# Batch 0's gate/up products switch to block products two units earlier, and a unit's five weight sums come from three VectorE operations

## The reference

```
base = x W^T                                   (1024 -> 1024)
y    = base + 2 * (x A_e^T * gates) B^T        (8 experts of rank 16, top 2 by biased logits)
gate = y Wg^T ; up = y Wu^T                    (1024 -> 3584)
h    = silu(gate) * up
out  = x + h Wd^T                              (3584 -> 1024)
```

## Time and profile before

| | |
|---|---|
| median of three runs | 1322.58 us (1322.0 to 1322.73) |
| span of the profiled execution, first to last instruction | 1320.3 us |
| median less that span | 2.3 us |
| PE busy | 1315.4 us, 8592 matmuls |
| DVE busy | 801.2 us (61%) |
| ACT, POOL busy | 405.1 us, 118.4 us |
| granted TensorE clock | 9 in all 40 slices of the page |
| moved by DMA | 287.58 MB |

### The profile page before, as it was taken

How to read it: one execution, slowest core, us unless ns; L and a number is a source line. 1 busy time by engine, 2 the same in 40 slices (tenths; PEclk the granted TensorE clock), 3 DMA queues, 4 the chain that set the end, 5 groups by cost and what they waited for, 6 DMA issues and landing times.

```text
span 1320.3 us, 22272 instructions
## 1 busy us (share of the span) xinstructions
PE 1315.4 (100%) x8592; PEld 863.2 (65%) x8592; DVE 801.2 (61%) x1581; ACT 405.1 (31%) x703; POOL 118.4 (9%) x156
## 2 busy tenths in 40 slices
PE   9999999999999999999999999999999999999999
PEld 7854566546666666676667666667666766666666
DVE  7889898788525587763733455555473254545613
ACT  4377755461102343421101233332110122222000
POOL 3200011150000011100000101100000011111000
PEclk9999999999999999999999999999999999999999
DMA  8479977216946788843884668553387355556564
GB/s 294 154 267 359 371 288 256 78 65 238 347 148 184 252 308 320 325 147 113 278 296 152 221 210 274 181 156 121 110 315 269 131 188 183 181 180 212 171 233 135
DMA packets 119609, 287.58 MB, mean 218 GB/s; under 512 B 15184, under 2 KB 18896, under 8 KB 118736
## 3 DMA queue, kind: packets, MB, share of 16 engines
q1 hardware_dynamic: 119216, 285.99, 62.7%
q10 hardware_dynamic: 288, 0.16, 0.0%
HBM read 241.80 MB, written 44.30 MB: 217 GB/s over the span
## 4 chain that ended last, share of the span: by engine, by line
PE 96%; DVE 2%; DMA 1%; issue 0%; SPq 0%; ACT 0%; DVEq 0%
PE banks L1072 26%; PE banks L1025 23%; PE banks L1095 14%; PE banks L1102 13%; PE banks L815 4%; PE banks L867 2%; PE banks L994 2%; PE banks L993 2%; PE banks L911 1%; PE banks L912 1%; PE banks L913 1%; PE banks L908 1%; PE banks L909 1%; PE banks L910 1%; PE banks L1131 1%; DMA mix_dram<-mixed 1%
## 5 line engine op out<-in xcount | busy, mean ns | idle before, releaser
L1072 PE MATMUL banks<-y_hi,gu_ring 128*128 128x512 f16 x1552 | 365.4, 379 | 0.0
L1072 PEld LDWEIGHTS banks<-y_hi,gu_ring 128*128 128x128 f16 x1552 | 151.8, 98 | 143.5
L1095 PE MATMUL banks<-h,piece 128*128 128x512 f16 x840 | 188.5, 379 | 0.0
L2031 ACT ACTIVATE sg<-banks,sc 128x512 f32<-128x512 f32 x112 | 76.8, 687 | 226.5 <-DVE banks L1757 165.4
L2272 POOL TENSOR_TENSOR m<-m,m 128x256 f32<-128x256 f32 x100 | 72.6, 726 | 821.2 <-DVE m L1738 815.1
L1095 PEld LDWEIGHTS banks<-h,piece 128*128 128x128 f16 x840 | 82.2, 98 | 89.8
L1760 DVE TENSOR_TENSOR banks<-banks,m 128x256 f32<-128x256 f32 x100 | 43.1, 431 | 133.5 <-PE banks L1072 133.3
L1102 PE MATMUL banks<-h,piece 128*128 128x256 f16 x896 | 106.2, 273 | 0.0
L1102 PEld LDWEIGHTS banks<-h,piece 128*128 128x128 f16 x896 | 87.7, 98 | 19.7
L1025 PE MATMUL banks<-y_lo,gu_ring 128*128 128x256 f16 x776 | 100.6, 273 | 0.0
L2159 ACT COPY m<-banks 128x256 f32<-128x256 f32 x100 | 36.8, 368 | 169.2 <-PE banks L1025 169.1
(11 more groups left out here) (258 smaller groups left out, 2006.8 us busy)
## 6 DMA issues: line engine op xcount, KB each, us to landing
piece<-down_dram SPq DMA_DIRECT2D x80, 448.0 KB, 5.8
mix_c<-mix_dram SPq DMA_DIRECT2D x84, 384.0 KB, 3.9
piece<-Wd SPq DMA_DIRECT2D x64, 448.0 KB, 5.5
gu_ring<-Wg SPq DMA_DIRECT2D x108, 256.0 KB, 3.2
gu_ring<-Wu SPq DMA_DIRECT2D x108, 256.0 KB, 3.0
mix_a<-mix_dram SPq DMA_DIRECT2D x84, 256.0 KB, 2.7
mix_dram<-mixed SPq DMA_DIRECT2D x28, 640.0 KB, 5.6
wb<-w_dram SPq DMA_DIRECT2D x64, 256.0 KB, 3.4
```

What stands on the lines that cost most here:

```text
L1072: mm = MM(bank, w[:, k, :], y_hi[:, k, :], start=False, stop=(k == KC - 1), skip_group_check=True)
L1095: mm = MM(bank, w[:, k, :], h[:, half * MH + k, 0, :], start=(start and k == 0), stop=False, skip_group_check=True)
L2031: S.activation(sg[:, n % SG, :], banks[:, chunk_bank(b, m, 0), :], ACT.Silu, scale=sc[:, b, 1:2]).then_inc(s_sg, 1)
```

## The change

- `PLAIN` becomes 10: units 10 and 11 of batch 0 go by block products too.
- `SUM_AT` is spread anew. Before, the sums of (units) were at s: 0:(0) 1:(1) 2:(2,3) 3:(4) 4:(5) 5:(6) 6:(7) 7:(8,9) 8:(10) 9:(11) 10:(12,13) and from 11 on s:(s+3). Now: 0:(0) 1:(1) 2:(2,3) 3:(4) 4:(5) 5:(6,7) 6:(8) 7:(9) 8:(10,11) and from 9 on s:(s+3).
- `weight_sums` has three additions or subtractions: one of 128x512 and two of 128x1024. For that the order of the last two sums is swapped and product 6's sum has the other sign (a1-b1), which `y_sum[:, 1]` takes up with a factor of -2. So the doubling of `y_sum` (one operation of 128x3072, in every batch) becomes two, of 128x2x1024 and 128x1024.

```
-    PLAIN = 12
-    SUM_AT = {0: (0,), 1: (1,), 2: (2, 3), 7: (8, 9), 10: (12, 13)}
-    SUM_AT.update({s: (s + 1,) for s in range(3, 7)})
-    SUM_AT.update({s: (s + 2,) for s in range(8, 10)})
-    SUM_AT.update({s: (s + 3,) for s in range(11, MC - 3)})
+    PLAIN = 10
+    SUM_AT = {0: (0,), 1: (1,), 2: (2, 3), 3: (4,), 4: (5,), 5: (6, 7), 6: (8,), 7: (9,), 8: (10, 11)}
+    SUM_AT.update({s: (s + 3,) for s in range(9, MC - 3)})
...
-                    fifth, seventh, sixth = (mix(n)[:, i] for i in range(2, 5))
+                    fifth, sixth, seventh = (mix(n)[:, i] for i in range(2, 5))
...
-                step(V.tensor_scalar(y_sum[:], y_sum[:], 2.0, None, ALU.mult))
+                step(V.tensor_scalar(y_sum[:, 0:3:2], y_sum[:, 0:3:2], 2.0, None, ALU.mult))
+                step(V.tensor_scalar(y_sum[:, 1], y_sum[:, 1], -2.0, None, ALU.mult))
...
                 even, odd = halved[:, 0], halved[:, 1]
-                a1, a2, b1, b2 = (w[:, i * KC // 2:(i + 1) * KC // 2] for w in (odd, even) for i in range(2))
+                left, right = (halved[:, :, i * KC // 2:(i + 1) * KC // 2] for i in range(2))
                 out = mix(s)
-                V.tensor_tensor(out[:, 0], a1, b2, ALU.add)
-                V.tensor_tensor(out[:, 1], b1, b2, ALU.add)
-                V.tensor_tensor(out[:, 2], a1, a2, ALU.add)
-                V.tensor_tensor(out[:, 3], a2, b2, ALU.subtract)
-                V.tensor_tensor(out[:, 4], b1, a1, ALU.subtract).then_inc(s_mix, 1)
+                V.tensor_tensor(out[:, 0], odd[:, 0:KC // 2], even[:, KC // 2:KC], ALU.add)
+
+                V.tensor_tensor(out[:, 1:3], left, right, ALU.add)
+
+                V.tensor_tensor(out[:, 3:5].rearrange("p c k j -> p (c k) j"), odd, even,
+                                ALU.subtract).then_inc(s_mix, 1)
```

More of the change, by code:

```diff
@@ L1057, in products_576 @@
                 if n < MC:
-                    fifth, seventh, sixth = (mix(n)[:, i] for i in range(2, 5))
+                    fifth, sixth, seventh = (mix(n)[:, i] for i in range(2, 5))
                 else:
                     pe.wait_ge(d_mix_c[n % 2], 16 * ((n - MC) // 2 + 1))
-                    fifth, seventh, sixth = (mix_c[:, n % 2, i] for i in range(3))
+                    fifth, sixth, seventh = (mix_c[:, n % 2, i] for i in range(3))
                 pe.wait_ge(s_34, nth(n))
```

## The result

The changed kernel takes 1324.47 us in the median of 18 runs (1323.09 to 1326.33), the kernel before 1321.97 us in 18 runs beside them (1321.55 to 1323.15). Forecast were 1325.2 us and a range from 1322.8 to 1327.0. The spans of the two profiled executions are 1322.4 and 1320.3 us. One thing in the times was not foreseen: those of before scatter over 1.6 us, those of after over 3.2 us.

A forecast was written before the change was run, and what follows sets the result against it. PE was taken as the bound, busy 1315.4 of 1320.3 us. Units -0.80, waits +3.29, +0.20, +0.27, old waits -0.21, -0.14 gave +2.6 us on 1322.6: 1325.2 us, range 1322.8 to 1327.0.

The forecast's parts named there:

- Part 1: Units 10 and 11 of batch 0 by block products: PE gains 0.80 us, 6.51 us a unit against 6.91.
- Parts 2 and 3: On DVE, a unit's sums get 0.14 us cheaper; the doubling of y_sum costs 0.19 us more once a batch.
- rival (b): DVE isn't late at the switch, as wide operations cost like narrow ones: -1.2 us, 1321.4 us; chance 6%.
- Part 4: At the new switch DVE starts y_blocks at 138.39, 2.6 us late, and PE stands 1.39 us.
- Part 5: At m45 of unit 10, unit 9's store, landing at 142.8, holds unit 12's sums: PE 3.29 us late with y_blocks' wait.
- part 7: Old waits for m45: the 0.21 us at 156.09 goes, the one at 195.53 shrinks by 0.14 us.
- Part 6: The next two units: PE waits 0.20 us for m45 of unit 11, then 0.27 us for ACT's copy.
- rival (a): Unit 9's store is in time, waits are 1.64 + 0.20 + 0.27: +0.96 us, 1323.5 us; chance 20%.
- rival (d): After PE's new waits the clock falls to 1.2 GHz for one unit: 6.5 us longer, 1331.7 us; chance 3%.
- (c): The DMA backlog doesn't drain, sums of units 13 and 14 wait too: +5.6 us, 1328.2 us; chance 11%.

The follow-up runs named there:

- e1: The kernel before with only the three-operation sums and the new doubling of y_sum, block products still from unit 12: 1321.68 us.
- e5: The changed kernel with unit 12's sums in a spare buffer and one down sum moved from step 8 to 9: 1323.20 us.
- e10: e9 with DVE making m45 of unit 10 ahead of unit 12's sums in step 9: 1323.22 us.
- e12: e9 with block products from unit 12 and the spread of the sums as in the kernel before: 1321.70 us.
- e6: The changed kernel with the last 1.75 MB of Wd issued two steps later, behind unit 9's store and unit 12's load: 1322.89 us.
- e2: The changed kernel, switch at unit 10, but with five operations of 128x512 for a unit's sums as before: 1325.51 us.
- e3: The changed kernel with unit 12's sums written to a spare buffer, so that they wait for no store: 1324.15 us.
- e4: The changed kernel with one down sum moved from step 8 to 9, and the next ones spread anew: 1324.23 us.
- e11: e6 with three operations into an unused buffer on DVE ahead of y_blocks of batch 0: 1325.83 us.
- e9: e8 with ACT taking its copies (copy_12) ahead of the silu in even steps of batch 0: 1321.48 us.
- e8: e6 with two down sums moved behind the switch to block products, and the later ones spread anew: 1321.79 us.

## Why the prediction was right

The time came out 0.7 us under the forecast, and the waits came where they were said to come. Of these 0.7 us, 0.6 lie in the starting point: the sum was put on 1322.6 us, from three runs of the kernel before, and the median of its 18 runs is 1321.97. As a difference, +2.5 us stand against +2.6. So good a match is partly luck, since one large term was off and two causes were not in the sum.

**Part 1, 0.80 us for two units.** It holds as far as it can be read: block units are 6.51 us apart in after, and the lost starts less the 0.74 us of before, and less 0.80 where the switch is at unit 10, meet the medians of e1, e5 to e10 and e12 within 0.4 us (e6: 2.60 - 0.74 - 0.80 = +1.06, measured +1.0). In e2, e3, e4, e11 and after the median lies 0.5 to 0.8 us off, to either side: these are the kernels whose landings or clock differ most between executions.

**Parts 2 and 3.** The value between the two bounds was right: 0.60 us for the 1024-wide sum, 2.27 us for a unit, 0.69 and 0.43 us for the doubling. That refutes rival (b), and the profile of e1 shows both parts at once.

**Part 4.** DVE was at the switch within 0.01 us of the forecast, and PE lost 1.40 us there, 1.39 predicted. This is the largest term of the result, and it came from adding up DVE's queue from a point that stays, where it waits for PE.

**Part 5** failed in size. The second wait was to be 1.9 us and PE lost 1.06. The forecast took the label of 0.21 us off to find when PE wants `m45`; the lost start there was 0.38, so the term should have been 2.07 us (the same 0.17 us is missing in part 7, and the sum is not changed by it). From 2.07 to 1.06 it is the store, which landed 1.0 us before the time taken. The idle stretch of the DMA engines that I counted on came (share 0.44 in the slice from 118 us, and 0.70 over 115.47 to 120.47, where the same 5 us of before have 0.85) and still this store was no later. The traces of after, e2, e3, e4 and e5 put this landing between 141.8 and 143.7 us, so 142.8 was a fair middle and a single number the wrong form: the profile of after shows one draw. What the term lacked was unit 12's load: in the profiles of e3 and e4 it held DVE for 1.5 and 1.6 us, in that of after it did not.

**Part 6** held: 0.19 us for `m45` of unit 11 (0.20), and 0.37 us for the copy (0.27 predicted; its label says 0.21).

**Part 7.** The wait that went was worth 0.38 us, not 0.21, because its label leaves out the overlap of matmuls. The other lost 0.14 us, as said (0.37 to 0.23).

**The sum** by lost starts is -0.80 + 1.40 + 1.06 + 0.19 + 0.37 - 0.38 - 0.14 = +1.70 us for the profiled execution, where +2.6 was forecast; that is at the lower edge of what the prediction calls its forecast (+1.6 to +3.6), close to rival (a). The medians differ by 2.5 us, more than that. Two causes can make up the 0.8 us: landings later than in this profile, which the traces of e2 to e4 show and no trace of after does, and the clock, which is rival (d). It had 3% and one price, 6.5 us for all runs or none. In truth it struck 5 of 18 runs, at about 2 us each if they are like the profiled ones of e4 and e11. The 13 runs at 1.000 have a median of 1324.02 us, 0.45 below that of all 18 and 2.05 above before. How the 0.8 us divides is not settled by this, since executions with a late landing may be the ones in which the clock falls. So the forecast's nearness to 1324.5 owes something to an omission that stands against a landing taken late.

**The rivals.** (a), the store in time, is what e6 made: +1.0 us measured, +0.96 worked out. For after itself it was false. (c), a backlog that doesn't drain, did not come: from unit 13 on no DMA holds DVE's sums in any of these profiles.

## What to carry to other kernels

When an engine is a microsecond late at a fixed point, add up its queue from the last place where it truly waited; that gave 0.01 us of error here. When the DMA engines are full, look at what stands ahead of the transfer that is needed, and move what nobody needs yet behind it: one line was worth 1.5 us and two thirds of the scatter. And a saving on the bound engine is only worth what the next engine can follow: here 0.80 us of matmul time came down to 0.1 us by the lost starts of e9 and e12 (0.2 us by their medians), since DVE's work a unit had grown to the length of the unit.

## What the runs showed of the hardware

- A label of 0.21 us before a matmul stood for 0.38 us of lost time, and delays up to 0.27 us (`m45` in e1 and e8) carried no label. Start-to-start distances (0.216 us for 512 columns, 0.109 for 256) tell them.
- Waits of PE of 2.94 us (e4) and 3.43 us (e11) were followed by 3 to 7 us at half the clock in the profiled executions; the same two kernels kept 1.000 in other runs, e11 in three of six. Waits of 1.24 and 0.89 us in after's profile, of 1.25 and 1.88 us in e3's, and of 2.09 and 1.00 us in e2's were not.
- With the DMA engines busy (share 1.00 from 125 to 142 us in after), a transfer of 640 KB took 11.0 to 12.9 us to land in four executions with the same transfers ahead of it, issued at the same time. With 1.75 MB less in front it took 6.2 to 8.2 us in six (e6 to e11). The loads did not always land in the order of issue: in the trace of before one of unit 12's, issued after Wd's second row, landed at 137.0, Wd's at 138.0. The Trainium skill (DMA: Bandwidth & Descriptors, section Queues, rings and completion order) says that completion isn't first in, first out, and this agrees; these stores of a unit's sums landed in their order in each trace that I read for them.
